# Expert slots of a routed feed-forward kernel: 48 whole slots and 20 mixed ones of 32-row pieces in place of 79 whole slots

## The reference

```python
h = layernorm(x)                                   # 8192 tokens
top_vals, top_idx = top_k(h @ router_w.T, 1)       # one of 16 experts per token
s = sigmoid(top_val)
gate, up = split((h * s) @ gate_up_proj[e])        # e = the token's expert, 128 -> 2 x 128
routed = (up * silu(gate)) @ down_proj[e]          # 128 -> 128
shared = silu(h @ shared_gate_w.T) * (h @ shared_up_w.T) @ shared_down_w.T   # 128 -> 512 -> 128
out = x + shared + routed
```

## Time and profile before

| | |
|---|---|
| median of 3 runs | 490.42 us |
| the profiled execution | 490.73 us |
| its span in the trace | 488.6 us |
| outside the span | 2.1 us |
| mean granted clock of PE | 0.999 of full speed |
| busy shares | PE 98%, PEld 79%, DVE 76%, POOL 72%, ACT 66% |
| first load of a slot issued by SP | 349.82 us from the span's start |
| last product of PE over | 483.94 us |

### The profile page before, as it was taken

How to read it: one execution, slowest core, us unless ns; L and a number is a source line. 1 busy time by engine, 2 the same in 40 slices (tenths; PEclk the granted TensorE clock), 3 DMA queues, 4 the chain that set the end, 5 groups by cost and what they waited for, 6 DMA issues and landing times.

```text
span 488.6 us, 10463 instructions
## 1 busy us (share of the span) xinstructions
PE 477.0 (98%) x3093; PEld 388.2 (79%) x3093; DVE 371.1 (76%) x1056; ACT 323.8 (66%) x623; POOL 352.3 (72%) x573
## 2 busy tenths in 40 slices
PE   8999999999999999999999999999999999999995
PEld 7655777868777778686777867888899999999995
DVE  7889899899999998997899989747445555555535
ACT  2667887978978879777687886554365555555521
POOL 6655688898888988986788777677236676667750
PEclk9999999999999999999999999999999999999999
DMA  7007001102101011020101101111389854442028
GB/s 238 2 1 281 22 12 56 54 13 66 33 34 65 24 45 54 12 67 21 46 25 41 45 1 44 45 44 37 117 197 225 226 158 136 145 139 76 24 52 294
DMA packets 33031, 39.33 MB, mean 80 GB/s; under 512 B 4913, under 2 KB 29113, under 8 KB 32720
## 3 DMA queue, kind: packets, MB, share of 16 engines
q1 hardware_dynamic: 26640, 24.98, 17.8%
q0 software_dynamic: 5760, 13.16, 7.8%
q10 hardware_dynamic: 576, 0.52, 0.3%
HBM read 21.69 MB, written 17.93 MB: 81 GB/s over the span
## 4 chain that ended last, share of the span: by engine, by line
PE 77%; DVE 6%; issue 5%; POOL 5%; DMA 4%; ACT 2%; SPq 1%; POOLq 0%; DVEq 0%; ACTq 0%
PE bank L427 17%; PE bank L420 9%; PE bank L444 6%; PE bank L414 4%; PE bank L822 3%; PE bank L823 3%; PE bank L815 3%; PE bank L435 3%; PE bank L528 3%; PE bank L514 3%; PE bank L540 3%; PE bank L524 3%; PE bank L519 3%; PE bank L688 2%; PE bank L697 2%
## 5 line engine op out<-in xcount | busy, mean ns | idle before, releaser
L427 PE MATMUL bank<-hT,wm 128*128 128x256 f32 x512 | 124.7, 383 | 0.6 <-ACT kr L908 0.6
L427 PEld LDWEIGHTS bank<-hT,wm 128*128 128x128 f32 x512 | 92.0, 190 | 18.7 <-issue 8.3
L1528 POOL DMA_INDIRECT sorted_rows<-rows,posi x64 | 71.9, 1124 | 19.6 <-issue 16.9
L1612 POOL DMA_INDIRECT out<-shared x55 | 53.2, 967 | 37.3 <-DVE shared L1442 22.3
L420 PEld LDWEIGHTS bank<-wm,k 128*128 128x128 f32 x512 | 61.7, 192 | 7.6 <-issue 6.6
L420 PE MATMUL bank<-wm,k 128*128 128x128 f32 x512 | 62.1, 275 | 0.0
L1084 ACT ACTIVATE er<-bank 128x256 f32<-128x256 f32 x40 | 15.4, 384 | 44.8 <-PE bank L823 44.3
L1450 DVE TENSOR_TENSOR e<-er,bank 128x256 f32<-128x256 f32 x40 | 16.9, 421 | 23.0 <-ACT er L1084 21.1
L444 PE MATMUL bank<-wm,actA 128*128 128x128 f32 x240 | 32.9, 280 | 0.0
L1612 POOL DMA_INDIRECT out<-rows x24 | 23.1, 964 | 11.3 <-DVE rows L1442 5.3
L944 ACT ACTIVATE h<-rows,smE 128x128 f32<-128x128 f32 x64 | 26.3, 482 | 6.7 <-POOL smE L1504 6.7
(11 more groups left out here) (256 smaller groups left out, 1293.9 us busy)
## 6 DMA issues: line engine op xcount, KB each, us to landing
shared<-sorted_rows SPq DMA_DIRECT2D x56, 128.5 KB, 2.9
shared<-x SPq DMA_DIRECT2D x16, 256.0 KB, 3.0
rows<-sorted_rows SPq DMA_DIRECT2D x24, 128.5 KB, 2.5
wexp<-w_exp SPq DMA_DIRECT2D x2, 1536.0 KB, 8.4
sorted_rows<-filler SPq DMA_DIRECT2D x17, 128.5 KB
shared<-out SPq DMA_DIRECT2D x6, 256.0 KB, 4.7
out<-shared SPq DMA_DIRECT2D x12, 128.0 KB, 2.7
sorted_rows<-rows,posi POOLq DMA_INDIRECT x64
```

What stands on the lines that cost most here:

```text
L427: ins = mm(dst[:, j * HALF:(j + 1) * HALF], W(name, 2 * pair_ + j), src[:, half * HALF:(half + 1) * HALF], start=True, stop=True)
L1528: g_.indirect_dma_start(sorted_ap, bass.IndirectOffsetOnAxis(posi[t % 3][:, g:g + 1].bitcast(U32), 0), rows[t % 3][:, g, :], None).then_in ...
L1612: g_.indirect_dma_start(out, bass.IndirectOffsetOnAxis(xr[k % RING][:, j, D:D + 1].bitcast(U32), 0), xr[k % RING][:, j, D + 1:ROW], None, ...
```

## The change

The slots are cut in two kinds. `UNI` = 48 whole slots hold full blocks of 128 rows. All other rows are cut into 80 pieces of 32 rows (`SUBS`), four to a mixed slot, each with an expert of its own; 20 mixed slots stand in ten of the 34 pairs: 5, 8, 11, ... 32 (`MIXED`). For a mixed pair SP issues 8 loads, ACT makes 8 weight copies, PE does 16 gate and up products of 32 columns in place of 4 of 128, and 8 down products whose weights are 32 columns wide and whose 128 columns move, into 32 of the 128 partitions each, in place of 2. Stores stay one per slot, those of mixed slots with a bound check. The 16 filler blocks have 32 rows, are all written ahead of pair 5's loads, and SP waits for them there. The weight copies go into 23 buffers, four copies a turn. The tables have 18 steps in place of 15, and their constants are made in a function of 10 operations of which none ran before, ahead of tile 2's `ew` (two constants of before go). ACT reads 32 words in place of 16. `LATE_AFTER` is 22: 27 late steps lie between the slots and 22 behind them.

```diff
-NS = NTOK // P + NE
-NP = NS // 2
+SUB = P // 4
+UNI = NTOK // P - NE
+SUBS = NTOK // SUB + NE - 4 * UNI
+NS = UNI + SUBS
+MIXED = range(5, 34, 3)
+NP = UNI // 2 + len(MIXED)
-PACK = 5
+PACK = 4
-        xw = [q, an, xn2T, th, rv]
+        xw = q + an + xn2T + th + rv + k2 + a + xa + kr[2:4] + h
-        TAB_ROWS = 15
+        TAB_ROWS = 18
-        STEPS_BEFORE, LATE_TURN, LATE_AFTER = 1, 4, 16
+        STEPS_BEFORE, LATE_TURN, LATE_AFTER = 1, 4, 22
+        def parts(k):
+            return 4 if k in MIXED else 1
+        def entry(k, j, c):
+            mixed = sum(1 for u in MIXED if u < k)
+            return UNI + 8 * mixed + 4 * j + c if k in MIXED else 2 * (k - mixed) + j
+        def copied(m):
+            return min(copies_to(NP - 1), max(copies_to(min(m, NP - 1)), 4 * (m + 1))) if m >= 0 else 0
...
 # SP
             for k in range(NP):
-                if k == FILL_PAIRS[0]:
+                first = entry(k, 0, 0)
+                if k == MIXED[0]:
                     tails = entries(SP_ENGINE, tail_i, 0, FILL_ROW - P, NE)
-                if k in FILL_PAIRS:
-                    sp.dma_start(sorted_ap[bass.ds(tails[k - FILL_PAIRS[0]], P), :], filler[:, :]).then_inc(s["fill_out"], 16)
-                if k == FULL_SLOTS // 2:
+                    for row in tails:
+                        sp.dma_start(sorted_ap[bass.ds(row, SUB), :], filler[0:SUB, :]).then_inc(s["fill_out"], 16)
                     sp.wait_ge(s["fill_out"], 16 * (NE + 1))
-                if at_ == 0 and k:
-                    first_rows[:] = entries(SP_ENGINE, row_i, 2 * k, FILL_ROW, LOADED)
+                if first % LOADED == 0 and first >= UNI:
+                    sub_rows[:] = entries(SP_ENGINE, row_i, first, FILL_ROW, LOADED)
+                elif first % LOADED == 0 and k:
+                    uni_rows[:] = entries(SP_ENGINE, row_i, first, FILL_ROW, LOADED)
...
                 for j in range(2):
+                    if k in MIXED:
+                        for c in range(4):
+                            sp.dma_start(xr[k % RING][c * SUB:(c + 1) * SUB, j, :],
+                                         sorted_ap[bass.ds(sub_rows[entry(k, j, c) % LOADED], SUB), :]).then_inc(s[loaded(k)[0]], 16)
+                    else:
...
 # PE
-                    for j in stores(k):
-                        ins = mm(grp(XDN_B[k % 2], j), grp(xact[k % 4], j), w_of(k, j, 2), start=True, stop=True)
+                    for j in range(2):
+                        for c in range(parts(k)):
+                            rows_ = slice(c * SUB, (c + 1) * SUB) if k in MIXED else slice(0, P)
+                            ins = mm(grp(XDN_B[k % 2], j)[rows_, :], grp(xact[k % 4], j)[:, rows_], w_of(k, j, c, 2),
+                                     start=True, stop=True)
...
-                    for j in stores(k):
-                        mm(grp(XGU_B[k % 2], j), w_of(k, j, 0), xhT(k, j), start=True, stop=True)
-                        ins = mm(grp(XGU_B[k % 2], 2 + j), w_of(k, j, 1), xhT(k, j), start=True, stop=True)
+                    for j in range(2):
+                        for c in range(parts(k)):
+                            rows_ = slice(c * SUB, (c + 1) * SUB) if k in MIXED else slice(0, P)
+                            mm(grp(XGU_B[k % 2], j)[:, rows_], w_of(k, j, c, 0), xhT(k, j)[:, rows_], start=True, stop=True)
+                            ins = mm(grp(XGU_B[k % 2], 2 + j)[:, rows_], w_of(k, j, c, 1), xhT(k, j)[:, rows_], start=True, stop=True)
...
 # ACT
+            def copy_weights(first, last):
+                for i in range(first, last):
+                    k, j, c = copy_of(i)
+                    if i >= len(xw):
+                        wait(act_e, "xDN", copy_of(i - len(xw))[0])
+                    af(xw[i % len(xw)][:, 0:EW], wexp[:, bass.ds(expert_of(words, entry(k, j, c)) * EW, EW)], ACT.Copy).then_inc(s["xw"], 1)
...
 # DVE, in one_round
                 for t in at(2):
+                    if t == 2:
+                        table_consts()
```

More of the change, by code:

```diff
@@ L117, in wait, with grp @@
                 eng.wait_ge(s[name], (count - 1) * PER[name] + (PER[name] if k is None or t not in of else k))
+        def grp(tile, g):
+            return tile[:, g * P:(g + 1) * P]
         wm = sb("wm", MAIN_COLS)
@@ L168, in program @@
         oh = ring("oh", 2, (G, NE), BF16)
[L170 to L173, removed]
+        start_of = sb("start_of", (2, NE))
+        cnt_i, blocks_i, blocks, ahead = sb("cnt_i", (2, NE), I32), sb("blocks_i", (2, NE), I32), sb("blocks", (2, NE)), sb("ahead", NE)
+        cum, whole, rest, left = sb("cum", 1 + 2 * NE), sb("whole", NE + 1), sb("rest", NE), sb("left", NE)
+        step_of, sums, sum2 = sb("step_of", 2 * NE), sb("sums", (2, 2 * NE)), sb("sum2", 2)
+        is_sub, sub4, sub16, place_a, place_b, place_u = (sb(n, 1) for n in ("is_sub", "sub4", "sub16", "place_a", "place_b", "place_u"))
+        place16, place4 = (grp(xa[0], i).rearrange("p (w k) -> p w k", k=PACK) for i in range(2))
+        place = sb("place", WORDS)
         rowm, eidc = sb("rowm", 1), sb("eidc", 1)
@@ L282, in entries, with copies_to, copy_of, stored @@
                 skip_runtime_bounds_check_because="the table's last step takes the minimum with this bound")[1]
-        def laps(i):
-            return len(range(i, NP, RING))
+        def parts(k):
[3 more added lines that the diff above has]
+            return UNI + 8 * mixed + 4 * j + c if k in MIXED else 2 * (k - mixed) + j
+        def copies_to(k):
+            return sum(2 * parts(u) for u in range(k + 1))
+        def copy_of(i):
+            k = next(u for u in range(NP) if copies_to(u) > i)
+            return k, *divmod(i - copies_to(k - 1), parts(k))
+        def copied(m):
+            return min(copies_to(NP - 1), max(copies_to(min(m, NP - 1)), 4 * (m + 1))) if m >= 0 else 0
         def loaded(k):
+            i, count = k % RING, sum(32 * parts(u) for u in range(k % RING, k + 1, RING))
+            return (f"xr_in{i}", count) if i < 8 else (f"x_in{i - 8}", 16 * (NT // XR) + count)
+        def stored(k):
             i, lap = k % RING, k // RING + 1
-            return (f"xr_in{i}", 32 * lap) if i < 8 else (f"x_in{i - 8}", 16 * (NT // XR) + 32 * lap)
-        def stored(k):
-            i, lap, none = k % RING, k // RING + 1, 16 if k == NP - 1 else 0
             if i < 8:
-                return f"xout{i}", 32 * lap - none
+                return f"xout{i}", 32 * lap
             if i == 11:
[L299 to L304, removed]
+                return "xout11", 32 * lap
+            return f"scat{i - 8}", 16 * G * len(range(i - 8, NT, 3)) + 32 * lap
         def late_sum(u):
@@ L322, in tl_sem @@
                 return "tl_in", 16 * (len(GP_LOADS) - 1)
-            return f"xr_in{u // 2}", 32 * laps(u // 2)
+            return loaded(max(range(u // 2, NP, RING)))
         def all_stored(eng):
@@ L349, in expert_of, with w_of @@
             return (words[slot // PACK] >> (slot % PACK * 4)) & (NE - 1)
-        def w_of(k, j, part):
-            return xw[k % XW][j][:, part * P:(part + 1) * P]
+        def w_of(k, j, c, part):
+            return xw[(copies_to(k - 1) + parts(k) * j + c) % len(xw)][:, part * P:(part + 1) * P]
         @block.sync
@@ L383, in _ @@
             sp.wait_ge(s["tab"], TAB_ROWS + 2)
[L384 removed]
+            uni_rows = list(entries(SP_ENGINE, row_i, 0, FILL_ROW, LOADED))
+            sub_rows = []
             sp.wait_ge(s["fill_out"], 16)
@@ L802, in one_turn @@
                     wait(pe, "xhT", k // 2 - 1)
-                    for i in [i for i in range(4) if i % 2 in stores(k + i // 2)]:
+                    for i in range(4):
                         if i % 2 == 0:
@@ L1068, in _ @@
             wait(act_e, "e", NT)
+            wait(act_e, "hs", NT)
             for u, step in late_order()[1:STEPS_BEFORE]:
                 late_step(u, step)
-            def one_turn(m):
[L1073 to L1077, removed]
+            def copy_weights(first, last):
[4 more added lines that the diff above has]
+                    af(xw[i % len(xw)][:, 0:EW], wexp[:, bass.ds(expert_of(words, entry(k, j, c)) * EW, EW)], ACT.Copy).then_inc(s["xw"], 1)
+            def one_turn(m):
+                copy_weights(copied(m - 1), (copied(m - 1) + copied(m)) // 2)
                 if m < NP:
@@ L1165, in tables @@
[L1165 to L1169, removed]
@@ new lines, in tables @@
+                tab(v.tensor_scalar(blocks_i[:, 0, :], cnt_i[:, 0, :], P.bit_length() - 1, None, ALU.logical_shift_right))
+                tab(v.tensor_scalar(blocks_i[:, 1, :], cnt_i[:, 1, :], SUB.bit_length() - 1, None, ALU.logical_shift_right))
+                tab(v.tensor_copy(blocks[:, :, :], blocks_i[:, :, :]))
+                tab(v.tensor_tensor_scan(ahead[:, :], one16[:, :], blocks[:, 0, :], 0.0, ALU.mult, ALU.add))
+                tab(v.tensor_scalar(cum[:, 1:1 + NE], ahead[:, :], float(UNI), None, ALU.min))
@@ L1606, in one_turn @@
```

(4 more changed lines are left out.)

58 lines of the change are left out of this document (32 added, 26 removed).

## The result

The changed kernel takes 528.04 us (median of 4 runs, 527.7 to 529.67) against 490.7 us beside it: 1.0768 times as long, 95% interval 1.0742 to 1.0794. The forecast was 526.6 us. The profiled execution takes 528.05 us, its span is 526.3 us, 37.7 more than before.

The account below looks back on a forecast made before the run. PE was taken as bound by the spacing of its own records. PE work +22.7, stall +12.5, clock +1.5, small terms +0.6 and +0.1, late steps -1.2 gave +36.2, 526.6 us; range 518 to 538.

Parts of the forecast that it names:

- Gate and up of the mixed slots: PE, 20 mixed slots: 16 records at the weight load's 0.112 us, +26.8 us; bounds 0 and +35.
- Down products: PE, ten mixed pairs: 16 narrow records at the router's 0.045 us plus switching, +4.5 us; bounds 0 and +13.4.
- Slots removed: PE: 79 slots become 68, each whole slot 0.78 us, saving 8.6 us.
- The fillers in SP's queue: SP ahead of pair 5's loads: 16 fillers delay them, PE stalls in turn 4, +12.5 us; bounds 4 and 15.
- the landing: SP's wait behind its last filler: issued about 364.2, store landing 2.7 us, perhaps 2.3, so done at 366.7.
- The clock: PE resumes at 1.2 GHz after idling some 12 us in turn 4, for 0 to 3 us: +1.5 us.
- the stall: PE in turn 4 waits for pair 5's loads from 361.5 to 374.1, 12.6 us, none regained.
- -0.3 at the start: Small terms: constants ahead of tile 2's `ew`, +0.6 us; three more table steps ahead of turn 0, +0.1 us.
- The late steps: Kernel's end: six more steps behind the slots cover the last stores and loads, -1.2 us; between 0.5 and 2.6.
- Cheap pieces on PE: First rival, PE's pieces: weight load hides, a 32-column product costs 0.027 us, total 499.9 us; chance 0.11.
- Cheap issues on SP: Rival, SP's queue: 32-row issues cost a quarter, stall is 4 us, clock stays, total 516.6 us; chance 0.09.
- Faster, with prices by rows: Rival, mixed turns and SP's queue: 32-row operations cost a quarter of 128-row ones, total 485.3 us; chance 0.03.

Follow-up runs that it names:

- the two runs that change one side alone: Changed kernel, gate and up of mixed pairs loading 32 of 128 weight columns: 500.29 us; changed kernel, pieces moving 128, 96, 64 and 32 columns: 523.01 us.
- narrow weights: Changed kernel with mixed pairs' gate and up products loading only 32 of 128 weight columns, giving 32 of 128 result rows: 500.29 us, a single run.
- shown in the kernel before: Kernel before with all 16 filler blocks, still of 128 rows, and the wait for them ahead of pair 5's loads: 504.51 us, ratio 1.0273.
- both kernels' times: Kernel before, LATE_AFTER 22: 489.16 us, 1.65 less; changed kernel with more columns moved, LATE_AFTER back at 16: 524.7 us, 1.7 more than with 22.
- both other kernels with more columns: Changed kernel with pieces moving 128 to 32 columns, plus fillers issued among the table steps: 515.1 us; or plus LATE_AFTER back at 16: 524.7 us.
- whole products, narrow down products kept: Changed kernel with one whole gate and up product each per mixed slot, other three pieces' left out, eight down products and copies kept: 497.12 us, single run.
- the fillers first: Changed kernel with filler rows computed first among the table steps and fillers issued at once, only their wait ahead of pair 5: 524.02 us, ratio 1.0645.
- 16 late steps: Changed kernel with LATE_AFTER back at 16, so 33 late steps between the slots: 534.23 us, ratio 1.0877.

## Why the prediction was right, and where it was off

The time lay 1.4 us above the forecast, inside the range, by the mechanism that was forecast; several terms were somewhat off, and one was missing. That the total came so close is in part luck, as the bullet on the clock shows.

- **Gate and up of the mixed slots**, +26.8 predicted, +26.0 measured. The choice between the bounds, the weight load, is shown by the two runs that change one side alone: fewer weight columns make it cheap, more moving columns cost nothing. The Trainium skill's page "TensorE: Matmul & The Clock Gate" has a number for each side. Its section "Back-to-back issue gap" gives some 60 cycles for 1 to 64 columns, which the prediction's first rival took; but that table is for a product by itself, and the section says that in a stream of loads and products both set the spacing. Its section "LDWEIGHTS (loading the stationary operand)" gives P / 1.2 ns for P weight columns, by estimate 107 ns for 128. The trace agrees with the load (0.109 us a record); with narrow weights a record took 0.035 us.
- **Down products**, +4.5 predicted, +3.3 measured: the four strips of partitions ran at 0.036 us a record, not the router's 0.045; the switches were right at 0.10 and 0.11.
- **Slots removed**, -8.6: nothing in the runs speaks against it, though no run took slots out alone.
- **The fillers in SP's queue**, +12.5 predicted, +10.6 measured. The step that was mis-sized is the landing: SP waited 1.2 us behind its last filler, where I had put 1.9 (364.8 to 366.7), and the pieces went out at 0.48, not 0.5, and had landed 5.4 us after the first issue, not 6.2. That hardly any of it is regained is shown in the kernel before: +13.3 for 14.3 of stall and cold turns.
- **The clock** behind the stall, +1.5 predicted, +2.5 measured, within its bounds of 0 to 3. What failed is that this was all of the clock: the prediction priced it only behind an idle PE. Behind mixed pairs it fell three times with no idle PE, 5.0 us. This is the missing term. The other errors (-0.8 - 1.2 - 1.9 + 1.0, -0.3 at the start, -0.6 at the end) make -3.8 and nearly cancel it, which is why the time came out close. That was luck: in other arrangements of the kernel the clock took up to 14.7 us.
- **The late steps**, -1.2 predicted; -1.8 at the end of the trace, -1.7 in both kernels' times.
- **The rivals.** Cheap pieces on PE: refuted by the records, 0.109 us and not 0.027. Cheap issues on SP: refuted, a load of 32 KB costs SP 0.48 us and a filler 0.53. Faster, with prices by rows: refuted with both.

## What to carry to other kernels

Before cutting a product into pieces, count the weight loads, not the moving columns: where the load already takes as long as the product (0.11 us each here), fewer columns save nothing, and each piece brings a load of its own. A batch of small DMAs costs the queue by their number; put it where the queue idles, and ask what stands behind its wait. Where a matmul engine is the bound, keeping independent work for the end, where the last transfers would otherwise be waited for, can pay by itself: 1.65 us here for one number.

## What had not been expected

The granted clock fell to 1.2 GHz while PE's records had no gap. What PE did before: all three falls of the changed kernel came as a mixed pair's 32 records ended, each 0.11 us of load and 32 moving columns, 3.5 us together. With 128 to 32 columns in the same 3.5 us it never fell in the slots behind the stall (1.00 over 120 us, and 1.00 in both other kernels with more columns). With narrow weights, where the stretch is 1.1 us, and with whole products, narrow down products kept, the two rows of the clock show no fall behind the stall either. How often it falls differs by arrangement and run: not behind every mixed pair, but three of ten in the changed kernel, for 5.0 us; 10.2 us were lost with the fillers first and 14.7 with 16 late steps. Its spread explains that the fillers-first kernel ranged from 518.57 to 524.88 us: the fastest run has a mean clock of 0.987, the others 0.977, some 5 us. The same page of the Trainium skill, section "HAM oscillation — how this bites in real kernels", tells of idle gaps as what brings the clock down; here the rows show falls without one, and none once the same 32 records moved 2.5 times the columns. Why it fell behind some mixed pairs and not behind others stays open. The remedy was odd: two and a half times the columns moved in the pieces' gate and up products, for the same result, made the kernel 5 us faster.
